# A perceiver block on one core: the products with the identity that open TensorE's work become rounds of sixteen 32 by 32 tile products

## What is computed

```
x = x + cross_attention(layernorm(x), ctx, bias; Wq, Wk, Wv, Wo)   # 16 heads, ctx is (4, 2048, 512)
x = x + hgrn_with_ternary_weights(layernorm(x); w_i, w_f, w_g, w_o, w_gate, w_down)
x = x + moe_top2(layernorm(x); Wr, br, W1, b1, W2, b2)             # 8 experts, hidden 2048
```

## Time and profile before

| | |
|---|---|
| time of three runs | 1005.37, 1005.64, 1005.93 us, median 1005.64 |
| span of the profiled execution | 1003.4 us, one core |
| what lies around the span, against the median of the runs | 2.2 us |
| TensorE busy | 970.8 us |
| VectorE, ScalarE, GpSimd busy | 599.4, 488.4, 258.3 us |
| mean granted clock of TensorE | 0.998 |

### The profile page before, as it was taken

The page is one execution under the profiler, slowest core; times in us unless marked ns, Lnnn a source line. Parts: engine busy times, 40 slices in busy tenths (PEclk is TensorE's granted clock), DMA queues, the critical chain, the costliest instruction groups (busy, mean ns, idle before and its releaser), DMA issues. The chain is left out here.

```text
span 1003.4 us, 18226 instructions
## 1 busy us (share of the span) xinstructions
PE 970.8 (97%) x7342; PEld 815.7 (81%) x7350; DVE 599.4 (60%) x1178; ACT 488.4 (49%) x633; POOL 258.3 (26%) x254
## 2 busy tenths in 40 slices
PE   9999999999999999999999999987899999999996
PEld 8888788888778888788888787554589999999995
DVE  6517895565886467886364886685652112455552
ACT  4211885171886155787051687578621102455551
POOL 2202830002840001850000760678400201111100
PEclk9999999999999999999999999999999999999999
DMA  8294861524771615781421787400079949699930
GB/s 293 71 192 85 179 153 46 212 84 120 176 171 49 275 42 168 173 199 46 164 83 48 173 177 267 157 2 0 33 270 382 373 165 332 227 381 345 336 110 13
DMA packets 77597, 169.92 MB, mean 169 GB/s; under 512 B 6473, under 2 KB 17609, under 8 KB 72385
## 3 DMA queue, kind: packets, MB, share of 16 engines
q1 hardware_dynamic: 75392, 163.87, 53.2%
q0 software_dynamic: 2112, 4.80, 2.1%
HBM read 119.01 MB, written 16.10 MB: 135 GB/s over the span
## 5 line engine op out<-in xcount | busy, mean ns | idle before, releaser
L995 POOL CAST stack<-kT 128x2048 fp32r<-128x2048 f32 x32 | 62.8, 1976 | 381.4 <-ACT kT L850 374.0
L712 DVE CUSTOM_DVE_ANT_0 prob<-psum,biasmap,top 128x512 f32<-128x512 f32 x192 | 144.2, 751 | 15.5 <-PE psum L482 7.0
L894 ACT ACTIVATE prob<-prob,top 128x2048 f32<-128x2048 f32 x64 | 128.7, 2010 | 37.7 <-DVE top L712 37.7
L2319 PE MATMUL psum<-xT,wring 128*128 128x128 f32 (+3 forms) x1024 | 133.9, 291 | 0.4 <-ACT xT L2673 0.4
L502 PE MATMUL psum<-ident,prob 128*128 128x128 f32 x1024 | 130.8, 274 | 1.3 <-ACT probT L902 1.3
L2319 PEld LDWEIGHTS psum<-xT,wring 128*128 128x128 f32 x1024 | 130.4, 191 | 1.8 <-ACT xT L2673 0.7
L502 PEld LDWEIGHTS psum<-ident,prob 128*128 128x128 f32 x1024 | 116.7, 140 | 16.0 <-issue 4.4
L850 ACT COPY kT<-psum 128x512 f32<-128x512 f32 x64 | 37.5, 585 | 188.9 <-PE psum L414 188.7
L429 PE MATMUL psum<-wv_hi,ctx_part 128*128 128x512 f32 x256 | 99.9, 390 | 0.1
L431 PE MATMUL psum<-wv_hi,ctx_part 128*128 128x512 f32 x256 | 99.7, 389 | 0.0
L430 PE MATMUL psum<-wv_lo,ctx_part 128*128 128x512 f32 x256 | 99.6, 389 | 0.0
(11 more groups left out here) (284 smaller groups left out, 1771.0 us busy)
## 6 DMA issues: line engine op xcount, KB each, us to landing
wring<-in_w SPq DMA_DIRECT2D x64, 1024.0 KB, 8.6
ctx_raw<-in_ctx_t SPq DMA_DIRECT2D x15, 1024.0 KB, 6.0
stack<-stack SPq DMA_DIRECT2D x32, 256.0 KB, 4.7
early_stack<-early_stack SPq DMA_DIRECT2D x28, 256.0 KB, 3.8
prob<-in_w_gate_t SPq DMA_DIRECT2D x1, 5632.0 KB, 17.5
stack<-key_stack SPq DMA_DIRECT2D x20, 256.0 KB, 4.0
query_stacks<-prob SPq DMA_DIRECT2D x16, 256.0 KB, 5.4
qstack<-query_stacks SPq DMA_DIRECT2D x16, 256.0 KB, 5.2
```

Of the source, the lines that this page charges most:

```text
L712: dve.tensor_tensor_reduce(prob[:, slot, keys], psum[:, scores.of[n, j, c], :], biasmap[:, keys], 1.0, top[:, h, (c + 1) % 2:(c + 1) % 2 + ...
L894: act.activation(prob[:, slot, :], prob[:, slot, :], ACT.Exp, bias=top[:, h, 1:2], scale=-1.0, accum_out=top[:, h, 2:3]).then_inc(*raised. ...
L2319: mm = pe.matmul(psum[:, w, 0:width], wring[piece][:, k, h % 4 * P:(h % 4 + 1) * P], xT[:, q % 2, k, 0:width], start=(k == 0), stop=(k == ...
```

## The change

TensorE: the ten products of the full identity are replaced by three rounds of sixteen products. In a round, `j` goes over the four groups of 32 rows of the array and `i` over the four groups of 32 columns; product (j, i) has the 32 by 32 block (j, i) of the identity as its stationary operand and streams the 32 rows `j` of the identity four times over, 512 columns in all (a broadcast access pattern), into the partitions of column group `i` of PSUM bank `j`. `tile_position` names the tile of the array. That makes 48 float32 products of 512 columns. `QUAD` is 4 and `DH` is 32. The results are read by nobody, as before.

VectorE: ahead of its first instruction it now waits for the identity, transposes it by blocks of 32 by 32 into `oT`, and waits for itself. Nobody reads that either; `oT` is written anew later.

```diff
--- before.py
+++ after.py
@@ -55,7 +55,7 @@
 WEIGH_LATER = 2
 TOGETHER = 2
 FILLERS = (2, 2, 2, 2, 2, 2, 2, 2, 2, 2)
-WARMING = 10
+WARMING = 3
 EARLY_KEYS = KEYS - CHUNK
 SUMS_AT = 5
 
@@ -550,7 +550,13 @@
             def project_first_keys():
                 pe.wait_ge(*constants.at("ident"))
                 for _ in range(WARMING):
-                    pe.matmul(psum[:, 0, 0:P], ident[:, :], ident[:, :], start=True, stop=True)
+                    for j in range(QUAD):
+                        for i in range(QUAD):
+                            rows_of_tile, columns_of_tile = slice(j * DH, (j + 1) * DH), slice(i * DH, (i + 1) * DH)
+                            pe.matmul(psum[columns_of_tile, j, :].rearrange("p (o n) -> p o n", o=QUAD),
+                                      ident[rows_of_tile, columns_of_tile],
+                                      ident[rows_of_tile, :].rearrange("p (o n) -> p o n", o=1).broadcast_to(
+                                          [DH, QUAD, P]), start=True, stop=True, tile_position=(j * DH, i * DH))
                 banks = [work.take(("keys", 0, 0, m), keys_copied.at(0, 0, m))[0] for m in range(DT)]
                 high = lambda k, m: wk_hi[:, k, m * P:(m + 1) * P]
                 low = lambda k, m: wk_lo[:, k, m * P:(m + 1) * P]
@@ -783,6 +789,9 @@
                 dve.tensor_tensor(x1[:, b, :], psum[:, wo_at[b], :], resid[:, b, :],
                                   ALU.add).then_inc(*x1_added.made(b))
 
+            dve.wait_ge(*constants.at("ident"))
+            dve.transpose(oT[:, :], ident[:, :]).then_inc(*own.made())
+            dve.wait_ge(*own.last())
             for k in range(DT):
                 dve.wait_ge(*slice_high.at(k, "wk"))
                 dve.tensor_tensor(wk_lo[:, k, :], wk_sb[:, k, :], wk_hi[:, k, :].bitcast(F32),
```

## The result

The changed kernel takes 1008.51 us in the median of five runs (1006.32 to 1010.69), the kernel before 1005.37 in five runs beside them: a ratio of 1.0032, 95% interval 1.002 to 1.0044. A second set, nine runs on another chip, gave 1008.76 against 1005.66, ratio 1.0029 (1.0019 to 1.0039). The change makes the kernel 3.1 us slower, 0.3%. The profiled execution took 1008.94 us, its span is 1007.2, 3.8 more than that of before.

A forecast was written before the change was run, and what follows sets the result against it. TensorE was taken to bound the kernel. Rounds ending at 6.45 plus 0.16 for tile shape put real products at 6.61 against 6.02, so 1005.64 + 0.59 = 1006.2 us, range 1005.0 to 1007.8.

The forecast's parts named there:

- the prediction's own border of 2.0 us: Whole kernel: a difference under 0.2%, or 2.0 us, counts as the same; slower than that was given 0.19.
- what the opening loses, the end loses: Whole kernel: TensorE works 970.8 of 1003.4 us, so real products starting d later make the end d later.
- the estimate from L517: Opening: L517's 32-column products run 3.5 of 4 at once; all sixteen tiles were taken to do so too.
- the rival of the later clock: Opening: small tiles don't count as work, so the clock rises near 11.6 us; +3.3 us, 1008.9; chance 0.09.
- The two rivals of tiles that take turns: Opening: row groups in turn, +8.3 us, 1013.9, chance 0.06; nothing at once, +39 us, 1045, chance 0.02.
- The change of tile shape: Opening, between tile rounds and first real product: going from tiles to the full array takes 0.16 us, bounds 0 and 0.3.
- The low part of the context: Opening, behind the transpose in VectorE's list: ready at 6.22 us and wanted about 0.9 later.
- Three rounds 5.16: Opening on TensorE: three tile rounds of 1.72 us each at the low clock take 5.16, ending at 6.45.
- the rival of the overlap with a loss: Opening: all sixteen tiles run at once but 1.35 times as long; +1.5 us, 1007.1; chance 0.08.
- 0.59 was forecast: Opening: real products start at 6.61 us against 6.02 before, with the clock up, a difference of +0.59 us.
- It costs nothing: Opening on VectorE: transpose and two waits, 0.28 to 0.69 us or four times that, end by 4.3 under idle time.
- for effects further down that I can't see: Later in the kernel: 0.03 taken off the same, 0.02 given to slower and 0.01 to faster.

The follow-up runs named there:

- e2: The changed kernel without VectorE's transpose and its waits, tile rounds alone: 1007.19 us, 1.9 over the kernel before.
- e1: The kernel before with only VectorE's block transpose and its waits added: 1006.34 us, 1.0 over the kernel before.
- e4: The kernel before with a one-column VectorE copy and the same waits, in place of the transpose: 1006.29 us, 0.6 over the kernel before.
- e5: The kernel before with two VectorE block transposes in a row and their waits: 1005.34 us, 0.3 under the kernel before.
- e9: The changed kernel with a second VectorE block transpose behind the first: 1007.51 us, 1.9 over the kernel before.
- e8: The changed kernel again, with no edit, nine runs on another chip: 1008.76 us, 3.1 over the kernel before.
- e13: The changed kernel with seven in place of four filling identity products near 730 us: 1007.36 us, 1.9 over the kernel before.
- e14: The changed kernel with a second block transpose and seven in place of four filling products near 730 us: 1006.58 us, 1.1 over the kernel before.
- e3: The kernel before with 14 opening identity products in place of ten: 1006.43 us, 1.1 over the kernel before.
- e10: The kernel before with six identity products more, behind the first chunk of keys: 1008.51 us, 2.9 over the kernel before.
- e7: The kernel before with 26 opening identity products in place of ten: 1008.99 us, 3.3 over the kernel before.
- e12: The kernel before with seven in place of four filling identity products near 730 us: 1005.32 us, 0.2 under the kernel before.
- e6: The changed kernel without the transpose and with two tile rounds in place of three: 1006.17 us, 0.5 over the kernel before.

## Why the prediction was wrong

Forecast 1006.2 within 1005.0 to 1007.8, "the same" at 0.80; measured 1008.5 to 1008.8, outside it, and slower by the prediction's own border of 2.0 us.

*What held.* TensorE bounds: what the opening loses, the end loses. The tiles run sixteen at a time, the second wave 0.86 behind the first; the estimate from L517, whose four column groups were all the trace could show, carried over to the row direction for the first two waves. The clock rises under tile products as under full ones (e2), so the rival of the later clock fails, though its 1008.9 is near the result: that is coincidence. The two rivals of tiles that take turns fail. The transpose and its waits are hidden where I said. The change of tile shape took no more than some 0.1 us. The low part of the context had 1.7 us to spare (ready at 6.22, wanted at 7.89), not the 0.9 of the prediction; nothing hung on it.

*"Three rounds 5.16": too short.* They took 5.85 (1.60 to about 7.45). The third and fourth waves stand 0.24 us late for all but one of their tiles, the fifth and sixth about 0.47, as L517's blocks of 1.01 in place of 0.87 us had hinted; I had this as the rival of the overlap with a loss. At the same moment of the clock's rise, the 1.61 us between 5.88 and 7.49 are worth half, 0.80 us; the traces of e1 and the changed kernel, with the rise at 7.45 and 7.38, are 0.9 apart, where 0.59 was forecast. The rest of the 1.54 in the profiled run, 0.65, is that its clock rose later than in the profile of before. This part is chance between two executions and no cost of the change.

The Trainium skill ("TensorE: Matmul & The Clock Gate", Part 3) gives a factor of 10.6 for sixteen tiles; by it the rounds would have taken 7.8 us, an estimate. Measured are 5.85, which is 82.6 / 5.85 = 14 tiles' worth, so here the measurement decides against the page's factor.

*"It costs nothing", on VectorE: the step that failed most plainly.* The work cost nothing. The instruction did: it moved instructions that TensorE waits for onto the places of VectorE's list where the engine pauses for about half a microsecond. e4 shows that what the instruction does is irrelevant, e5 and e9 that one more takes the cost away again. In the traces it is 0.65 us, between the medians of e8 and e9 1.25 and of e13 and e14 0.8. The pauses stay at records 447 and 959 of the list, and what differs is which instruction stands there. That they are fetches of instructions is my reading. For it speaks that the traces list DMA packets of the kind "instruction", and that in the five traces with the pause near 588 us one of 8 KB begins 1.1 to 1.3 us behind the pause; behind the one near 286 the next begins only 2.4 us later. No run varied this, so the cause of the pauses stays open.

*The 0.03 "for effects further down that I can't see": too little.* They are the dips of the clock near 730 us. The trace of before showed the thin stretch: filling, eight-column products, 0.65 us of idle, and its mean clock of 0.998. I took one execution's clean clock for the kernel's. Nearly four in ten runs of the kernel before have a dip as well; with the stretch 0.5 to 2 us later in their traces it is 5 to 9 in 10 (e1, e2, e3, e8, e9). e10 shows that a delay behind the opening does it too, e7 that 3.6 us later none came in six runs, e12 to e14 that filling the idle time takes most of it away. Taking the dips away is worth 1.25 us in the changed kernel (3.10 over before in e8, 1.85 in e13) and 0.2 in the one before (e12). In all eight traces with a dip it begins 720 to 727 us behind the clock's rise, so where it can fall seems tied to that rise, which is chance, and not to the program alone.

*The 3.7 us between the two profiled runs:* opening 0.9, later rise of the clock 0.65 (chance), moved pauses 0.65, dip 0.97, wait for the gather 0.57.

*The 3.1 us between the medians, by parts:* opening 1.26 (e14 over e12), moved pauses 0.78 (e13 over e14), dips 1.25 - 0.19 = 1.06 more than before has. The three make up 3.10 because each is a difference to the next, so their sum proves nothing. Each rests on medians of 9 to 12 runs that spread over 2 us and more, and by resampling these runs the first could be anything from 0.8 to 1.8, the second from 0.2 to 2.1, and the third from nothing to 1.7. The opening's 1.26 is above the 0.9 of the traces and within that. Open: why e6 doesn't gain, what brings the wait near 764 us, and what the rhythm is in which the dips come.

## What to carry to other kernels

In a kernel that one engine bounds and that is timed to a part in a thousand, an instruction hidden under idle time isn't free until its effect on the rest of that engine's list is seen: compare the starts of the bounding engine's records all along both traces and look at each step up. Before a delay of a microsecond is put down as only that, look for thin stretches of TensorE's work further down and at the mean granted clock of several runs, since one profiled execution can show a clean clock where more than every third run dips. When two traces differ in the opening, look first at when the clock rose in each. Products that only keep TensorE busy are best put into idle time in front of such a stretch; at the very start, how long they last counts, not how they fill the array.

## What the runs showed of the hardware that was not expected

- Sixteen 32 by 32 tiles in float32 start within 0.11 us, and each product's two records stand one wave apart (0.85 us at the low clock for 512 columns); in the second round one record starts on time and the other fifteen 0.24 us later, and in the third most are 0.24 us later again.
- VectorE pauses for some 0.35 us more than usual (gaps of 0.41 and 0.48 us) in front of records 447 and 959 of its list in all five traces with one added instruction, whatever that does. TensorE pauses for 0.59 to 0.65 us without a waiting reason in e3 and e10, with 8 and 12 matmul records more ahead of the place, and not in the kernel before.
- The clock rises to its high level between 4.8 and 7.6 us after the start, from one execution to another; in e1 against the profile of before that alone moved all later work by 0.65 us.
- The granted clock fell to 1.2 GHz for about a third of 10 us (0.83) in a stretch where TensorE was busy over 80% of the time by its records, with small products and the identity. The share of runs with such a dip was 49 of 128 with the stretch where the kernel before has it, 8 of 9 some 2 us later, and 0 of 6 some 3.6 us later.
- VectorE's block transpose of 128 by 128 in float32 takes 0.31 us.
